# Token stage of a two-branch transformer block: value and LoRA columns regrouped, LoRA transposes halved, head strips

## The reference

```python
Q, K = elu(heads(xn @ wq.T + bq)) + 1, elu(heads(xn @ wk.T + bk)) + 1
V = heads(xn @ wv.T + bv)                      # 16 heads of 32
KV, K_sum = sum_s K^T V, sum_s K
attention = (Q KV / (Q K_sum + 1e-8)) @ wo.T + bo

w = top-2 of 8 experts: sigmoid(xn @ W_router) (ranked with expert_bias), normalised
gate = xn @ W_gate + lora_shared + sum_e w_e * (xn @ A_e @ B_e) / 8       # rank 8
up   = the same with the up matrices
ffn  = h @ W_down + lora_shared + lora_experts(h),  h = silu(gate) * up    # 1376 wide
```

## Time and profile before

| | |
|---|---|
| median of 3 runs | 714.65 us (712.37 to 715.01) |
| the profiled execution | 714.12 us, span 712.3 us |
| PE busy | 695.2 us, 98% of the span |
| DVE, ACT, POOL busy | 379.2, 259.1, 121.9 us |
| chain that ended last | PE 90%, DVE 4%, issue 2%, POOL 2%, ACT 1%, DMA 1% |

### The profile page before, as it was taken

The page is one execution under the profiler, slowest core; times in us unless marked ns, Lnnn a source line. Parts: engine busy times, 40 slices in busy tenths (PEclk is TensorE's granted clock), DMA queues, the critical chain, the costliest instruction groups (busy, mean ns, idle before and its releaser), DMA issues.

```text
span 712.3 us, 10760 instructions
## 1 busy us (share of the span) xinstructions
PE 695.2 (98%) x3668; PEld 560.9 (79%) x3668; DVE 379.2 (53%) x724; ACT 259.1 (36%) x401; POOL 121.9 (17%) x293
## 2 busy tenths in 40 slices
PE   7999999989999998999999999999999999999997
PEld 6788888876766766888888888888888888888886
DVE  5566655676766774544434544434644434644434
ACT  3344433564422413423324333324333323333322
POOL 2454455421624615000000000000000000000000
PEclk9999999999999999999999999999999999999999
DMA  7856667234545353500001500001500001300001
GB/s 228 314 196 214 213 210 249 90 148 188 214 178 218 110 215 108 188 0 0 0 0 60 231 6 0 0 0 59 225 11 0 0 0 59 118 0 0 0 0 60
DMA packets 23044, 73.17 MB, mean 103 GB/s; under 512 B 2720, under 2 KB 3104, under 8 KB 20976
## 3 DMA queue, kind: packets, MB, share of 16 engines
q1 hardware_dynamic: 22848, 72.61, 28.6%
q0 software_dynamic: 176, 0.30, 0.2%
HBM read 51.93 MB, written 20.97 MB: 102 GB/s over the span
## 4 chain that ended last, share of the span: by engine, by line
PE 90%; DVE 4%; issue 2%; POOL 2%; ACT 1%; DMA 1%; SPq 0%; DVEq 0%; POOLq 0%; ACTq 0%
PE bank L1129 20%; PE bank L1131 19%; PE bank L1130 19%; PE bank L1355 17%; PE bank L1330 6%; PE bank L1243 2%; PE bank L1343 1%; PE bank L1341 1%; DMA w_raw<-in_wkT 1%; PE bank L1194 1%; PE bank L1146 1%; PE bank L1166 1%; PE bank L1158 1%; PE bank L1251 1%; PE bank L1294 0%
## 5 line engine op out<-in xcount | busy, mean ns | idle before, releaser
L1129 PE MATMUL bank<-x,up_h 128*128 (+1 forms) x352 | 137.2, 390 | 2.1 <-DVE qf L997 1.2
L1130 PE MATMUL bank<-x,up_h 128*128 (+1 forms) x352 | 137.2, 390 | 0.0
L1131 PE MATMUL bank<-x,up_l 128*128 (+1 forms) x352 | 137.1, 389 | 0.0
L1065 DVE TENSOR_TENSOR hf<-bank,silu 128x512 f32<-128x512 f32 x44 | 30.4, 691 | 155.9 <-issue 136.2
L1355 PE MATMUL bank<-dn,hid_h 128*128 128x512 f32 x352 | 108.8, 390 | 0.0
L1129 PEld LDWEIGHTS bank<-x,up_h 128*128 128x128 f32 x352 | 66.1, 188 | 19.0 <-issue 2.1
L607 ACT ACTIVATE hid_h<-hf 128x512 fp32r<-128x512 f32 x44 | 27.8, 632 | 141.8 <-DVE hf L1065 141.8
L1130 PEld LDWEIGHTS bank<-x,up_h 128*128 128x128 f32 x352 | 66.1, 188 | 14.2
L1131 PEld LDWEIGHTS bank<-x,up_l 128*128 128x128 f32 x352 | 66.1, 188 | 13.8
L1355 PEld LDWEIGHTS bank<-dn,hid_h 128*128 128x128 f32 x352 | 65.8, 188 | 13.8
L801 DVE TENSOR_TENSOR up_l<-up_raw,up_h 128x1024 fp32r<-128x1024 f32 x45 | 55.6, 1235 | 31.0 <-ACT up_h L607 31.0
(11 more groups left out here) (164 smaller groups left out, 1164.8 us busy)
## 6 DMA issues: line engine op xcount, KB each, us to landing
x<-scr_x SPq DMA_DIRECT2D x8, 2048.0 KB, 7.6
up_raw<-in_ffn_up SPq DMA_DIRECT2D x11, 768.0 KB, 5.8
scr_x<-xt SPq DMA_DIRECT2D x16, 512.0 KB, 4.8
xin<-in_x SPq DMA_DIRECT2D x16, 256.0 KB, 5.8
scr_z<-zt SPq DMA_DIRECT2D x16, 256.0 KB, 2.2
x3r<-in_x SPq DMA_DIRECT2D x16, 256.0 KB, 3.7
scr_att<-x3r SPq DMA_DIRECT2D x16, 256.0 KB, 2.2
z<-scr_z SPq DMA_DIRECT2D x4, 1024.0 KB, 4.9
```

Source lines behind the costliest of these rows:

```text
L1065: nc.vector.tensor_tensor(hf[:], ps_u[:], silu[:], ALU.mult).then_inc(h_done, 1)
L1129: nc.tensor.matmul(dst, lh, rh, start=start, stop=False, **kw)
L1130: nc.tensor.matmul(dst, lh, rl, start=False, stop=False, **kw)
L1131: return nc.tensor.matmul(dst, ll, rh, start=False, stop=stop, **kw)
```

## The change

1. **Values and LoRA columns.** The value weights and the 152 LoRA and router columns become one array of 664 columns per 128 rows (`va_h`, `va_l`), multiplied in two parts: 384 value columns, then the last 128 value columns with the 152. ACT copies the values in two parts.
2. **LoRA path.** DVE writes the weighted columns once to `zst`, two tiles behind instead of one, with no split; PE makes two transposes instead of four, now behind the value columns; ACT copies the transposed float32 into `zt` with two instructions, and `lora_lo` on DVE makes the low rows there, with two instructions on 64 partitions by 256. `zt_done` comes from DVE and no longer from ACT. `zraw` has two halves.
3. **DVE's order in a tile**: the key sum, `compare`, the next tile's low tokens, the weighting, statistics, `select`, `kf`, `normalise`, `zraw`, `lora_lo`. ACT splits the next tile's tokens first. POOL computes the deviation three tiles ahead, between `rank` and the sum of weights.
4. **Head strips.** `denominators` writes each channel chunk to its own 32-row strip of the bank (4 heads, twice), and `expand` reads 32-row strips into four banks, all four in one place. `kcur` holds both batch elements, made by POOL from `kvacc`. `rr` covers 128 rows; DVE makes the low rows by a mask.
5. **Edges.** The loop has five passes and four tiles are written out behind it; `wo` is split a quarter per tile in tiles 12 to 15, its last low quarter after the stage. `sa_dn` is loaded after the stage. The last group's `split_up` is cut in two around `attention`.

```diff
-        ps_xt, ps_k, ps_kv, ps_v, ps_z, ps_zt = bank[0], bank[1], bank[2], bank[4], bank[5], bank[6]
-        ps_q, ps_den, ps_exp, ps_att = [bank[0], bank[1]], bank[2], [bank[4], bank[5]], [bank[6], bank[7]]
+        ps_xt, ps_k, ps_kv, ps_zt = bank[0], bank[1], bank[2], bank[6]
+        ps_va, ps_vz = bank[4][:, 0:VA], bank[5][:, 0:P + NZ]
+        ps_z = bank[5][:, P:P + NZ]
+        ps_q, ps_den, ps_exp, ps_att = [bank[0], bank[1]], bank[2], bank[2:6], [bank[6], bank[7]]
...
-            with eng.Fori(0, TILES // 2 - 2) as p:
+            with eng.Fori(0, TILES // 2 - 3) as p:
...
-            for t in range(TILES - 2, TILES):
+            for t in range(TILES - 4, TILES):
                 body(t, t // 2, t % 2)
...
+            sp.wait_ge(kf_done, TILES)
+            sp.dma_start(sa_dn[:], dram["sa_dn"]).then_inc(sa_in, 16)
...
+                if more:
+                    rstd_of(t + 3)
...
+            def key_sums(b):
+
+                pool.wait_ge(kvacc_done, (b + 1) * TB // 2 + 1)
+                tt(kcur[:, b], hcol[:], kvacc[:, b, :, DK:AUG].to_broadcast([P, KD, DK]), ALU.mult).then_inc(kcur_done, 1)
+
+            pool.wait_ge(s2_in, 16 * STAGE2_LOADS)
+            key_sums(0)
+            route(TILES - 2, more=False)
+            route(TILES - 1, more=False)
+            key_sums(1)
...
-            def lora_hi(t):
-
-                act.wait_ge(zf_done, t + 1)
-                round_to(zst[:, :, :, 0:ER], zf[:].unsqueeze(2).to_broadcast([P, 2, 2, ER]))
-                round_to(shared_cols(zst), zs[:].unsqueeze(2).to_broadcast([P, 2, 2, R])).then_inc(zhi_done, 1)
-
             def lora_out(t):
                 act.wait_ge(zt_ready, t + 1)
                 act.wait_ge(scr_zd, 16 * (t + 1))
-                round_to(zt[:].rearrange("p k n -> p (k n)"), ps_zt[:]).then_inc(zt_done, 1)
+                pst = ps_zt[:, 0:2 * P].rearrange("p (a n) -> p a n", a=2)
+                round_to(zt4[:, :, 1], pst)
+                round_to(zt4[0:ER, :, 0], pst[0:ER]).then_inc(zhi_done, 1)
...
+                if ahead(t, 1):
+                    tokens_hi(t + 1, 1 - s, half + s)
...
+                act.wait_ge(va_ready, t + 1)
+                round_to(vf[:, s, 0:KD - 1, :, 0:DK], ps_va.rearrange("p (k h n) -> p k h n", h=HC, n=DK)).then_inc(va_done, 1)
+                if isinstance(t, int) and t in WO_PART:
+
+                    k = WO_PART[t]
+                    act.wait_ge(s2_in, 16 * STAGE2_LOADS)
+                    round_to(wo_h[:, k], w_raw[:, 0, k]).then_inc(woh_done, 1)
+
+                act.wait_ge(zraw_done, t + 1)
+                round_to(vf[:, s, KD - 1, :, 0:DK], ps_vz[:, 0:P].rearrange("p (h n) -> p h n", n=DK)).then_inc(vf_done, 1)
+                nc.scalar.activation(rexp[:], zraw[:, s, NZ - E:], ACT.Exp, scale=-1.0).then_inc(rexp_done, 1)
                 if behind(t, 2):
                     lora_out(t - 2)
...
-            def lora_weighted(t):
+            def lora_weighted(t, s):
                 dve.wait_ge(route_done, t + 1)
...
+                wait(dve, zt_ready, t)
+                shared = zraw[:, s, 2 * ER:2 * ER + 2 * R].rearrange("p (a o r) -> p a o r", a=2, o=1)
+                nc.vector.tensor_scalar(zst[:, :, SH:].rearrange("p a (b c) -> p a b c", c=2 * R)[:, :, 0:3, 0:R],
+                                        shared.to_broadcast([P, 2, 3, R]), RSCALE, None, ALU.mult)
                 weight = wtok[:, bass.ds(t, 1), :].unsqueeze(3).to_broadcast([P, 1, E, R])
                 for a in range(2):
                     last = nc.vector.tensor_tensor(
-                        zf[:, a:a + 1].rearrange("p a (e r) -> p a e r", e=E),
-                        zraw[:, a * ER:(a + 1) * ER].rearrange("p (a e r) -> p a e r", a=1, e=E), weight, ALU.mult)
-                last.then_inc(zf_done, 1)
+                        zst[:, a:a + 1, 0:ER].rearrange("p a (e r) -> p a e r", e=E),
+                        zraw[:, s, a * ER:(a + 1) * ER].rearrange("p (a e r) -> p a e r", a=1, e=E), weight, ALU.mult)
+                last.then_inc(zst_done, 1)
             def lora_lo(t):
-                dve.wait_ge(zf_done, t + 1)
+
                 dve.wait_ge(zhi_done, t + 1)
-                stack_lo(zst, zf, zs).then_inc(zst_done, 1)
+                pst = ps_zt[:, 0:2 * P].rearrange("p (a n) -> p a n", a=2)
+                sub(zt4[ER:, :, 0], pst[0:ER], zt4[0:ER, :, 0])
+                nc.vector.scalar_tensor_tensor(zt4[ER:, :, 1], zt4[ER:, :, 1].bitcast(F32), zmask[ER:], pst[ER:], ALU.mult, ALU.add
+                                               ).then_inc(zt_done, 1)
...
+                dve.wait_ge(k_ready, t + 1)
+                wait(dve, kf_done, t)
+                nc.vector.tensor_tensor(kb[:], ps_k[:], bk_b[:], ALU.add).then_inc(kb_done, 1)
                 if not first:
                     compare(t - 1)
-                    select(t - 1)
...
-                dve.wait_ge(k_ready, t + 1)
-                nc.vector.tensor_tensor(kb[:], ps_k[:], bk_b[:], ALU.add).then_inc(kb_done, 1)
-                if first:
-                    tokens_lo(1, 1)
+                if ahead(t, 1):
+                    tokens_lo(t + 1, 1 - s)
+                if behind(t, 2):
+                    lora_weighted(t - 2, s)
                 if ahead(t, 2):
                     stats_of(t + 2, s, half + 1)
-                else:
-
-                    for k in WO_HALF[t]:
-                        dve.wait_ge(woh_done, k + 1)
-                        sub(wo_l[:, k], w_raw[:, 0, k], wo_h[:, k]).then_inc(wol_done, 1)
+                if isinstance(t, int) and t in WO_PART and t > TILES - KD:
+                    k = WO_PART[t] - 1
+                    dve.wait_ge(woh_done, k + 1)
+                    sub(wo_l[:, k], w_raw[:, 0, k], wo_h[:, k]).then_inc(wol_done, 1)
+                if not first:
+                    select(t - 1)
                 dve.wait_ge(kexp_done, t + 1)
                 nc.vector.scalar_tensor_tensor(kf[:, s, :], kb[:], 0.0, kexp[:], ALU.max, ALU.add).then_inc(kf_done, 1)
-                if ahead(t, 1) and not first:
-                    tokens_lo(t + 1, 1 - s)
                 if isinstance(t, int) and t == TILES - 2:
                     heads_of(0)
-                if not first:
-                    lora_weighted(t - 1)
                 if ahead(t, 2):
                     normalise(t + 2, s)
-                if not first:
-                    lora_lo(t - 1)
-                dve.wait_ge(z_ready, t + 1)
-                nc.vector.tensor_copy(zraw[:], ps_z[:, 0:NZ]).then_inc(zraw_done, 1)
+                dve.wait_ge(vz_ready, t + 1)
+                if behind(t, 2):
+                    dve.wait_ge(zst_done, t - 1)
+                nc.vector.tensor_copy(zraw[:, s], ps_z).then_inc(zraw_done, 1)
                 if s == 0 and not first:
                     key_values(t - 1, half - 1)
+                if behind(t, 2):
+                    lora_lo(t - 2)
...
-            def group(g, first=False, then=None):
+            def group(g, first=False, last=False):
                 if not first:
                     queries(g, (1, 2, 3))
-                    shared_down(g, FC - (GROUPS - 2) * SHG if then is not None else SHG)
-                    attention(g - 1, (0, 1))
-                if then is not None:
-                    then()
+                    shared_down(g, FC - (GROUPS - 2) * SHG if last else SHG)
+                    attention(g - 1, (0,))
+                    if last:
+                        split_up_w(0, 0, 1).then_inc(upl_done, 1)
+                    attention(g - 1, (1,))
                 dve.wait_ge(den_ready, g + 1)
-                nc.vector.tensor_scalar(den[0:HEADS, :], ps_den[0:HEADS, :], EPS, None, ALU.add).then_inc(dene_done, 1)
+                nc.vector.tensor_scalar(den, ps_den[:], EPS, None, ALU.add).then_inc(dene_done, 1)
                 dve.wait_ge(dene_done, g + 1)
-                nc.vector.reciprocal(den[0:HEADS, :], den[0:HEADS, :]).then_inc(rden_done, 1)
+                nc.vector.reciprocal(den, den).then_inc(rden_done, 1)
                 dve.wait_ge(rden_done, g + 1)
                 dve.wait_ge(rrh_done, g + 1)
-                sub(rr[DK:DK + HEADS, :], den[0:HEADS, :], rr[0:HEADS, :]).then_inc(rr_done, 1)
+                nc.vector.scalar_tensor_tensor(rr[:], rr[:].bitcast(F32), lomask[:], den, ALU.mult, ALU.add
+                                               ).then_inc(rr_done, 1)
                 if first:
                     dve.wait_ge(scr_zd, 16 * (TILES + 1))
                 else:
                     attention(g - 1, (2, 3))
+                if last:
+                    split_up_b(0, 0).then_inc(upb_done, 1)
...
-                    nc.vector.tensor_tensor(qf[:, c, :], qf[:, c, :], ps_exp[c % 2][:], ALU.mult).then_inc(qn_done, 1)
+                    nc.vector.tensor_tensor(qf[:, c, :], qf[:, c, :], ps_exp[c][:], ALU.mult).then_inc(qn_done, 1)
                 for c in range(KD):
                     if c == 2 and first:
```

(40 more changed lines are left out.)

169 lines of the change are left out of this document (75 added, 94 removed).

## The result

The changed kernel takes **704.63 us** (median of 4 runs, 701.38 to 704.88); the kernel before, run beside it, 714.62 (712.37 to 715.01). The ratio is 0.9851, 95% interval 0.9832 to 0.9870: faster by 1.5%, more than the 0.5% that can be told here, and by half of what was forecast (694.0, range 688 to 702). The profiled execution took 704.41 us, span 702.6, against 714.12 and 712.3 before.

A forecast was written before the change was run, and what follows sets the result against it. PE's work was taken to bound the kernel, except between the stages, where chains count. Token stage 11.1, between stages 0, denominators 7.4 and expansion 1.65 sum to 20.15 us off 714.12, giving 694.0 us, range 688 to 702.

The forecast's parts named there:

- Joint columns: Every token-stage tile: 384 + 280 columns instead of 512 + 152 gain 0.43 us a tile, 6.9 in all, ends 0 and 9.0.
- Two transposes fewer: Token stage, 14 tiles from 2 on: two LoRA transposes fewer gain 0.18 us each tile, 2.5 us in all.
- Tile 2's wait: Start of token stage: PE's wait for DVE's low tokens at tile 2 goes, a gain of 1.5 us.
- The tile at 7.78: Token stage: PE still sets the pace, and a tile falls from 8.39 to 7.78 us.
- DVE's ring: Token stage: DVE's work plus its waits for ACT and POOL sum to 7.35 us a tile, under PE's 7.78.
- The ring through SP: Token stage: late token stores on SP delay reuse of xt; 15.35 us per two tiles against PE's 15.6, costed at nothing.
- the slower rival: Token stage: token stores land in 11.4 us in six bursts, costing 26.7 us, so 720.7 us; chance 0.03.
- Between the stages: From token stage to attention: gains 4.65 us and losses 4.7 cancel to 0, ends -3 and +3.
- The rival of the low clock: Between the stages: half rate carries into the twelve matmuls of the first queries, 2.4 us, so 696.4 us; chance 0.10.
- Denominators: Attention groups 1 to 3: four products on column strips take 1.07 us instead of 3.54, 2.47 each, 7.4 in all.
- Expansion: Attention groups 1 to 3: four products on row strips take about one pair's time, gaining 0.55 each, 1.65 us in all.
- The last group: Last attention group: cutting split_up in two trades one wait for another, gain 0.

The follow-up runs named there:

- e6: The changed kernel with e4's order on SP and the joint columns as 512 + 152 again, as in e3: 701.73 us, ratio 0.9831 to the kernel before.
- e4: The changed kernel with every token store issued one tile sooner on SP, right behind the x load: 698.10 us, ratio 0.9769 to the kernel before.
- e12: e5 without four of the twelve products of the last 280 columns in each tile, at less precision: 689.54 us, ratio 0.9655 to the kernel before.
- e1: The changed kernel with tile 1's token store issued on SP ahead of the wo and wq loads: 700.78 us, ratio 0.9793 to the kernel before.
- e2: The changed kernel with group 1's token load issued on SP ahead of tile 15's LoRA store: 701.88 us, ratio 0.9805 to the kernel before.
- e3: The changed kernel with the joint columns as 512 + 152 again and V evicted in one copy: 705.34 us, ratio 0.9856 to the kernel before.
- e5: The changed kernel with the SP moves of e1, e2 and e4 together: 693.17 us, ratio 0.9706 to the kernel before.

## Why the prediction was half right

- **Joint columns, 6.9:** right for a tile. The block gave 0.52 where the estimate was 0.43, in PE's pace 0.435 (e6 against e4). In the profiles of e4 and e6 they bring 6.2 us from K of tile 0 to K of tile 15; e6 has 0.7 of it back by an earlier start and 0.5 between the stages, so 5.0 are left at the end. Spacings 0.175 and 0.129 us, forecast 0.18 and 0.136: the 152 row was a floor, as taken.
- **Two transposes fewer, 0.18:** 0.13 with the step to the next product (0.79 us before, 0.66 after), so 1.8 us rather than 2.5.
- **Tile 2's wait, 1.5:** right; K of tile 2 gained 2.4.
- **The tile at 7.78:** 7.83. **DVE's ring at 7.35:** at most 7.33 (e12).
- **The ring through SP, costed at nothing. This step failed.** Inside the loop it held: PE waited for no store there, with a landing of at most 7.1 expected. But the sum was made for the steady loop only. The one store known to land in over 11 us was put into the slower rival as a thing that would have to happen in six bursts; it was never asked what it would do where it was already known to happen. There tile 3's split had been in time only because ACT came to it later: the store landed at 33.5 and the split started at 35.27, while the changed kernel could have split at about 30.2, as e1 does. Price at the start 3.5 us (e1). Tile 12's store, last of six issues, landed in 8.5 us, and tile 13 took 1.4 more than in e4. The two together are, within 0.2, the 4.7 missing at tile 15.
- **Between the stages, 0 with ends of 3:** it came out at -3.5 against the forecast. The list of losses was right in kind. Group 0's load cost 1.20 (2.0 taken); the profile files that wait under issue, but the load landed 8.8 us behind 140.68, at 149.5, and the queries start at 149.61. Group 1's load cost 1.64 (0.9 taken). The wait for the last quarter of wo was 2.8 with 1.7 at the keys by values before it, where 0.9 was taken. Two of the gains were not there in full. The wait for qf (1.6) stayed: PE waits 1.10 and 0.91 us for evicted queries where it had waited 1.56. Of the first denominators' 2.5 only 1.6 arrived, since DVE's chain behind them wasn't hidden: PE waits 0.66 us for rr.
- **The rival of the low clock, 2.4 us, chance 0.10:** in the changed kernel's profile it did not come true where it was named. The twelve first queries take 2.94 us, as before (2.97), and the six products ahead of them run at the half clock (0.59 from 145.5 to 149.6 us) as they had before (2.70 us for six, now 2.90 beside the wait). In the profiles of e1, e2 and e3 those queries did take 4.9 to 5.3. What the clock cost here is 1.36 us behind group 1's load (19.19 us to the denominators against 17.83 in e5), which belongs to the 2.25 missing at the end.
- **Denominators, 2.47 each:** 3.54 became 1.00. **Expansion, 0.55:** a group takes 25.12 us instead of 27.94, 2.82 less for 3.02 forecast, so the expansion is worth 0.28 net. **The last group, 0:** here PE now waits 1.47 us for the last qn_l. The chain from expansion through DVE and ACT to POOL, with 1.3 to 1.5 us a subtraction, did not get shorter with PE's work.
- The rule "the next thing late would be the xt store" was right, the forecast that its cover was enough was not. With three issues moved on SP the kernel takes 693.2 us, near the forecast's 694.0. That doesn't make the forecast right. e2's and part of e4's move also take away waits that the forecast had counted as losses: in e5 the stretch from K of tile 15 to group 1's queries gains 2.2 us where 0.6 was forecast, and what follows 8.2 where 9.05 was. Two errors meet there.

What stays open: how much of e2's 2.7 us is its own; why the half clock follows some pauses and not others of the same length; and why the profiled starts of one and the same startup code differ by up to 1.7 us.

## What to carry to other kernels

When the bounding engine's work gets shorter, go through every transfer that something waits for and compare its issue and landing with the new time of need, the start and the last burst too and not only the steady loop; a landing time known from one place belongs first to the sum for that place. An ordered DMA queue whose issuing engine blocks on a late semaphore delays everything behind it: put the stores that free a buffer ahead of the waits they don't need. Measure an edit's parts at the pace of the finished kernel: e3 alone would have said that 5 us of gain were 0.7. And do not price a half clock from one profile: look whether other profiles with the same pause have it.

## What the runs showed of the hardware

- At tile 3, a pause of PE of 2.02 us was followed by some 3 us at the half clock in the changed kernel (0.57 from 36 to 40 us), and one of 1.37 us in e2 by none. With its clock the first cost 3.5 us in all. The length of the pause alone does not decide: at group 1's first queries 1.64 us was followed by a mean of 0.57 (176 to 180 us), 1.86 in e3 by the full clock.
- The Trainium skill, page "TensorE: Matmul & The Clock Gate", section "Back-to-back issue gap", gives an isolated matmul 2.5 ns over its columns' time at the full clock. The rows here do not agree: 0.175 us for 384 columns, 15 ns over their 160, and 0.129 for 280, 12 over 117.
- Four float32 products with 32 x 512 results on column strips took 1.00 us together against 3.54 for four with 16 rows each in a row: the strips run side by side, for products that read one 128-row operand as well as for row strips (0.44 us from e5's expansion, four products, to the next queries, 166.18 to 166.62, where two had taken 0.57).
- A 512 KB store issued right behind two 1 MB loads on one queue took 11.9 us to land against 6.6 in the steady loop; issued 0.5 us sooner behind the same loads it had landed 1.9 us sooner (e4: ACT goes on at 31.79 instead of 33.65), and issued ahead of them it took 6.2 us (e1). The loads' own share and their order on the queue were not separated.
